# A six-layer decoder on one core: sigmoids ahead in the up pass, more key buffers in the product stage, and the end by token tiles

## The reference

```python
x = ln(x + linear_attention(x))
x = ln(x + cross_attention(x, ctx))
x = ln(x + ffn(x))
x = ln(x + metric_attention(x))          # causal, per head metric
x = ln(x + cosine_cross_attention(x, ctx))
x = ln(x + real(ifft(fft(x) @ w)) + bias)
# ffn: every qdq scales by the maximum of its whole tensor
x = act_qdq(x)
up = act_qdq(x @ w_up.T)                 # 256 -> 768
gate = act_qdq(x @ w_gate.T)
sig = round_u16(sigmoid(gate))
t = act_qdq(gate * sig)
v = act_qdq(t * up)
return v @ w_down.T
```

## Time and profile before

| | |
|---|---|
| Median of 3 runs | 1425.21 us (1424.16 to 1429.18) |
| The profiled execution | 1429.01 us, its span 1427.2 us |
| PE busy | 1249.9 us (88%), granted clock 0.95 |
| DVE, ACT, POOL busy | 1042.0 (73%), 516.8 (36%), 263.7 us (18%) |
| DMA | 107.86 MB, mean 76 GB/s |

### The profile page before, as it was taken

One profiled execution on the slowest core, in us unless ns is written; L12 is line 12 of the kernel. 1 busy time (PEld: TensorE's weight loads), 2 busy tenths in 40 slices (PEclk: granted clock), 3 DMA queues, 4 the chain that ended last, 5 costly groups with the idle time before them and its releaser, 6 DMA issues.

```text
span 1427.2 us, 18392 instructions
## 1 busy us (share of the span) xinstructions
PE 1249.9 (88%) x7324; PEld 832.9 (58%) x7324; DVE 1042.0 (73%) x1930; ACT 516.8 (36%) x605; POOL 263.7 (18%) x184
## 2 busy tenths in 40 slices
PE   7899999979899999722778999999999999998964
PEld 4465666656544544311555676867768686766553
DVE  3579889986345598996343687978878797968684
ACT  1334434434434567674011333332323323341320
POOL 0011111110000000043100321414142231414140
PEclk9999999999999999856889999999999999999998
DMA  5001000004651246495221110121111100000000
GB/s 211 15 16 31 30 31 30 16 15 126 210 199 59 74 167 216 154 391 178 86 96 54 44 52 31 33 73 37 59 54 52 39 15 28 26 24 23 1 15 15
DMA packets 47781, 107.86 MB, mean 76 GB/s; under 512 B 10704, under 2 KB 31312, under 8 KB 44240
## 3 DMA queue, kind: packets, MB, share of 16 engines
q1 hardware_dynamic: 43536, 104.59, 21.0%
q10 hardware_dynamic: 4160, 2.10, 0.5%
HBM read 62.64 MB, written 44.04 MB: 75 GB/s over the span
## 4 chain that ended last, share of the span: by engine, by line
PE 74%; DVE 15%; ACT 4%; issue 3%; DMA 2%; POOL 1%; SPq 0%; POOLq 0%; DVEq 0%; ACTq 0%
PE ps L1290 8%; PE ps L1350 7%; PE ps L1177 6%; PE ps L1025 6%; PE ps L1076 6%; PE ps L779 3%; PE ps L1323 3%; PE ps L1237 3%; PE ps L927 2%; PE ps L1261 2%; PE ps L852 2%; PE ps L1272 2%; PE ps L1367 2%; PE ps L870 2%; PE ps L1337 2%
## 5 line engine op out<-in xcount | busy, mean ns | idle before, releaser
L1350 PE MATMUL ps<-arena 128*128 128x256 f32 x512 | 120.0, 388 | 6.7 <-ACT arena L1775 6.7
L1290 PE MATMUL ps<-arena 128*128 128x512 f32 x256 | 117.6, 598 | 0.0
L1350 PEld LDWEIGHTS ps<-arena 128*128 128x128 f32 x512 | 98.5, 195 | 28.0 <-ACT arena L1775 10.2
L1802 POOL TENSOR_TENSOR arena<-arena 128x4 f32<-128x4 f32 x48 | 49.4, 1033 | 340.7 <-DVE arena L1957 340.7
L2283 DVE TENSOR_TENSOR arena<-ps,arena 128x2048 f32<-128x2048 f32 x32 | 73.3, 2291 | 41.5 <-PE ps L1237 41.0
L1863 POOL TENSOR_TENSOR arena<-arena 128x16 f32<-128x16 f32 x32 | 91.9, 2908 | 34.1 <-DVE arena L2312 34.1
L1177 PE MATMUL ps<-arena 128*128 128x256 f32 x384 | 89.3, 392 | 9.0 <-DVE arena L2236 6.7
L1177 PEld LDWEIGHTS ps<-arena 128*128 128x128 f32 x384 | 74.7, 197 | 20.2 <-issue 7.1
L1025 PE MATMUL ps<-arena 128*128 128x512 f32 x192 | 85.5, 602 | 1.2 <-ACT arena L1502 1.2
L1076 PE MATMUL ps<-arena 128*128 128x512 f32 x192 | 84.7, 595 | 0.0
L1290 PEld LDWEIGHTS ps<-arena 128*128 128x128 f32 x256 | 46.3, 190 | 48.2 <-issue 44.5
(11 more groups left out here) (262 smaller groups left out, 2621.8 us busy)
## 6 DMA issues: line engine op xcount, KB each, us to landing
v_scratch<-arena SPq DMA_DIRECT2D x7, 1536.0 KB, 12.7
arena<-v_scratch SPq DMA_DIRECT2D x7, 1536.0 KB, 6.8
up_scratch<-arena SPq DMA_DIRECT2D x6, 1536.0 KB, 7.3
arena<-up_scratch SPq DMA_DIRECT2D x6, 1536.0 KB, 10.2
vw_scratch<-arena SPq DMA_DIRECT2D x32, 256.0 KB, 3.9
arena<-x_scratch SPq DMA_DIRECT2D x16, 512.0 KB, 4.4
arena<-vw_scratch SPq DMA_DIRECT2D x8, 1024.0 KB
arena<-x SPq DMA_DIRECT2D x8, 512.0 KB, 5.3
```

The lines of the kernel that those rows point to most:

```text
L1290: last = mm(flat(p % 2), w["cos_wq"][:, k, p * P:(p + 1) * P], xt4[:, k], start=k == 0, stop=k == NC - 1)
L1350: last = mm(flat(2)[:, C:2 * C], cos_pt[:, p], cos_vw[:, par, p], start=p == 0, stop=p == NP - 1)
L1802: g.tensor_tensor(var[0], var[1], neghalf[:, 0:NT], ALU.pow)\
```

## The change

In the up pass, ACT rounds gate n and takes its sigmoid between the early and the late copies of up batch n - 1; before, the rounding came after the late copies and the sigmoid between the copies of batch n. Copies of value products move later, 13 to 15 into the product stage. The peak of t is taken ahead of that of up; the last up peak is taken in two halves.

In the product stage keys get three rows (the first over the value weights, no longer needed), a square in the same place, four staging tiles and PSUM banks of their own (`KEY_BANK`); the waits on `ck_stored` go from ACT, and POOL waits for all four before it clears the pads. ACT's and SP's orders change. The partition maximum of v is found by PE and DVE: DVE spreads the maximum over 128 columns, PE transposes them, DVE takes the maximum of a row.

In loop two's last batch, everything behind `cos_o_add` is done tile by tile, with four stores of 128 KB.

```diff
         late_ctx = ar.take(NC, B * TC)
         assert ar.at <= weights + 2 * NC * FF
         ar.at = keep + V_ORDER[0] * NF * T
-        krow = ar.take(2, INNER)
-        ksq = ar.take(INNER)
+        krow = [wv_all[:, 0:INNER], ar.take(INNER), ar.take(INNER)]
+        ksq = wv_all[:, INNER:2 * INNER]
+        spread = vst[:, 0:P]
+        kst = [ar.take(NP, P)]
         ar.at = keep + V_ORDER[1] * NF * T
-        kst = ar.take(NP, P)
+        kst += [ar.take(NP, P) for g in range(3)]
+        KEY_BANK = (1, 3, 6, 1)
...
+            load_up(2)
+            store_vw(13)
+            load_up(3)
+            store_v(0)
             store_vw(14)
-            load_up(2)
-            load_up(3)
-            store_vw(15)
-            store_v(0)
+            store_v(1)
             load_up(4)
-            store_v(1)
             load_up(5)
             store_v(2)
+            store_vw(15)
             load_up(6)
             store_v(3)
...
+                if b.last():
+                    for t in range(NT):
+                        wait_tile(sp, "y6_ready", t)
+                        sp.dma_start(out_rows[B - 1][:, t], y6[:, t]).then_inc(sig("y_stored", 16).sem, 16)
+                    return
...
-                if g >= 2:
-                    pe.wait_ge(ev("cos_k_scaled"), g - 1)
+                if g == 2:
+                    pe.wait_ge(ev("vw_copied"), 2 * NP)
+                if g == 3:
+                    pe.wait_ge(ev("cos_k_scaled"), 1)
...
+                        last = mm(flat(KEY_BANK[g] + half), late_ctx[:, k, g * P:(g + 1) * P],
...
             value_products(14)
-            value_products(15)
             key_rows(0)
             key_rows(1)
+            value_products(15)
+            key_rows(2)
             turn_keys(0)
-            key_rows(2)
             turn_keys(1)
             key_rows(3)
             turn_keys(2)
             turn_keys(3)
-
-
-            pe.wait_ge(ev("vw_copied"), 2 * NP)
+            pe.wait_ge(ev("cos_k_scaled"), 4)
+            pe.wait_ge(ev("peak_found"), QUANTIZED["v"])
+            tr(flat(7)[:, 0:P], spread, ident).then_inc(ev("peak_shared"), 1)
...
+            def last_turn(t):
+                wait_tile(pe, "y5_ready", t)
+                for c in range(NC):
+                    last = tr(flat(4 + t)[:, c * P:(c + 1) * P], y5[:, t, c * P:(c + 1) * P], ident)
+                last.then_inc(sig("cos_x_turned").sem, 1)
+
+            def last_spec(t):
+                wait_tile(pe, "cos_x_copied", t)
+                for k in range(NC):
+                    last = mm(flat(SPEC_BANK[t])[:, 0:C], xt5[:, k, t * P:(t + 1) * P], spec_m[:, k],
+                              start=k == 0, stop=k == NC - 1)
+                last.then_inc(sig("spec_done").sem, 1)
...
+                wait(pe, "cos_pt_copied", b, NT, NT)
+                last_turn(0)
+                last_turn(1)
+                wait(pe, "cos_scaled", b, NT, NT)
+                last_spec(0)
+                last_turn(2)
+                last_spec(1)
+                last_spec(2)
+                last_turn(3)
+                last_spec(3)
...
+                if b.last():
+                    last_rows(b)
+                    return
...
             gate_round(1)
+            ffn_sigmoid(1)
             ffn_copy_up(0, late)
             copy_spec_forward()
             ffn_copy_up(1, early)
-            ffn_sigmoid(1)
+            gate_round(2)
+            ffn_sigmoid(2)
             ffn_copy_up(1, late)
-            gate_round(2)
             copy_spec()
             ffn_copy_up(2, early)
-            ffn_sigmoid(2)
+            gate_round(3)
+            ffn_sigmoid(3)
             ffn_copy_up(2, late)
...
             ffn_copy_up(3, early)
-            ffn_sigmoid(3)
+            gate_round(4)
+            ffn_sigmoid(4)
             ffn_copy_up(3, late)
             copy_vw(8)
-            gate_round(4)
+            ffn_copy_up(4, early)
+            gate_round(5)
+            ffn_sigmoid(5)
+            ffn_copy_up(4, late)
             copy_vw(9)
...
             copy_vw(10)
-            gate_round(6)
+            ffn_copy_up(6, early)
+            gate_round(7)
+            ffn_sigmoid(7)
+            ffn_copy_up(6, late)
...
             copy_vw(12)
-            copy_vw(13)
...
-                if g == 0:
+                if g == 1:
                     act.wait_ge(moved("v_stored", 0), moved_before("v_stored") + 16)
                     wait(act, "v_ready", Batch(1))
-                if g >= 2:
-                    act.wait_ge(ev("cos_k_turned"), g - 1)
-                f(krow[:, g % 2], flat(1 + 2 * (g % 2), 2), ACT.Copy).then_inc(ev("cos_k_copied"), 1)
+                if g == 3:
+                    act.wait_ge(ev("cos_k_turned"), 1)
+                f(krow[g % 3], flat(KEY_BANK[g], 2), ACT.Copy).then_inc(ev("cos_k_copied"), 1)
...
-                f(ksq, flat(1 + 2 * (g % 2), 2), ACT.Square).then_inc(ev("cos_k_squared"), 1)
...
                     wait(act, "v_ready", Batch(2))
-                else:
-                    act.wait_ge(ev("ck_stored"), 16 * g)
-                f(kst.rearrange("p a b -> p (a b)"), flat(1 + 2 * (g % 2), 2), ACT.Copy, scale=gk)\
+                f(kst[g].rearrange("p a b -> p (a b)"), flat(KEY_BANK[g], 2), ACT.Copy, scale=gk)\
...
+                act.dma_start(ck_d[:, :, g * P:(g + 1) * P], kst[g]).then_inc(ev("ck_stored"), 16)
...
             copy_values(7)
+            ffn_round_up(0)
+            copy_vw(13)
+            ffn_round_up(1)
+            ffn_round_t(1)
+            copy_keys(0)
             copy_vw(14)
-            ffn_round_up(0)
-            ffn_round_up(1)
-            copy_vw(15)
-            ffn_round_t(1)
             ffn_round_up(2)
             ffn_round_t(2)
-            copy_keys(0)
             ffn_round_up(3)
+            copy_vw(15)
+            copy_keys(1)
             ffn_round_t(3)
             ffn_round_up(4)
-            copy_keys(1)
+            copy_keys(2)
             ffn_round_t(4)
             ffn_round_up(5)
             ffn_round_t(5)
             store_keys(0)
             ffn_round_up(6)
-            copy_keys(2)
             ffn_round_t(6)
             store_keys(1)
+            copy_keys(3)
             ffn_round_up(7)
-            copy_keys(3)
             ffn_round_t(7)
             store_keys(2)
             store_keys(3)
...
+                if b.last():
+                    wait_previous(act, "spec_done", b)
+                    for t in range(NT):
+                        wait_tile(act, "cos_x_turned", t)
+                        f(xt5[:, :, t * P:(t + 1) * P], flat(4 + t)[:, 0:C].rearrange("p (c n) -> p c n", c=NC), ACT.Copy)\
+                            .then_inc(sig("cos_x_copied").sem, 1)
+                    return
...
+            share_peak("t")
             share_peak("up")
-            share_peak("t")
...
-            share_peak("v")
 
 
             wait_all_moved(pool, "v_stored", 4, 3)
+            pool.wait_ge(ev("ck_stored"), 16 * 4)
...
+            def last_rstd(name, t):
+                rs = norms[name][2][:, t:t + 1]
+                wait_tile(pool, name + "_stats", t)
+                g.tensor_tensor(rs, rs, neghalf[:, 0:1], ALU.pow).then_inc(sig(name + "_rstd").sem, 1)
...
+                    if b.last() and t:
+                        last_rstd("cos", t - 1)
...
+                    last_rstd("cos", NT - 1)
...
+                if b.last():
+                    for t in range(NT):
+                        last_rstd("spec", t)
...
+                if name == "v":
+                    link(v.tensor_reduce(quant["v_all"], flat(7)[:, 0:P], AX.X, ALU.max))
...
+            def last_up_peak():
+                for n in range(2):
+                    wait(dve, "up_copied", Batch(B - 1), NF * (n + 1) // 2, NF)
+                    half = ffn_up[:, (B - 1) % 2].rearrange("p t j n -> p t (j n)")[:, :, n * FF // 2:(n + 1) * FF // 2]
+                    v.memset(spare, 0.0)
+                    link(v.tensor_reduce(quant["tmp"], half, AX.XY, ALU.max, apply_absolute_value=True))
+                    last = v.tensor_tensor(quant["up_max"], quant["up_max"], quant["tmp"], ALU.max)
+                    if n == 0:
+                        link(last)
+                last.then_inc(sig("up_peaked").sem, 1)
+                wait(dve, "up_peaked", Batch(B - 1))
...
-            up_peak(B - 1)
-            peak("up")
             t_peak(B - 1)
             peak("t")
+            last_up_peak()
+            peak("up")
+            scale("t", quant["t_raw"])
             scale("up", quant["x_scale"])
-            scale("t", quant["t_raw"])
...
-                if q in (2, 3, 5, 6):
-                    sum_keys((2, 3, 5, 6).index(q))
-            peak("v")
+                if q in (1, 2, 3, 5):
+                    sum_keys((1, 2, 3, 5).index(q))
+            v.tensor_copy(spread, quant["v_max"].broadcast_to([P, P])).then_inc(ev("peak_found"), 1)
...
+            def last_stats(name, t, rows):
```

(69 more changed lines are left out.)

28 lines of the change are left out of this document (11 added, 17 removed).

## The result

The changed kernel takes 1405.09 us (median of 4 runs, 1404.13 to 1406.1) against 1425.29 us on the same chip: ratio 0.9856, 95% interval 0.9838 to 0.9873, some 20.5 us. The forecast was 1398.7, range 1393 to 1406: the time lies inside, 6.4 us above the forecast. The profiled execution took 1406.1 us with a span of 1404.2.

A forecast was written before the change was run, and what follows sets the result against it. The prediction saw PE 88% busy, with holes in the product stage and the last 26 us. Gains of 16.4 us up to scale v and 10.1 at the end, taken from the median 1425.2, gave 1398.7 us, range 1393 to 1406.

The forecast's parts named there:

- What bounds the kernel: PE is busy 88% of the span; gains outside the loops come from two holes, product stage and last 26 us.
- Sigmoids ahead: Up pass: DVE no longer waits for sigmoids but 12.6 us for late copies; up scale at 590.0, gain 3.3 us.
- wait some 0.75 us each: Up pass: value products 9 and 11 wait for a vw copy; PE ends at 583.3, before DVE wants it (586).
- the block on ACT stops PE: Up pass rival, 4%: each of seven blocks of rounding and sigmoid stalls PE 5.5 us; time 1440.
- First product: Start of the product stage: at 592.8 against 597.6, a gain of 4.8 us that includes the sigmoids' 3.3.
- Product stage: First product to last v peak: 65.3 us for 61.6 of DVE work, ending at 658.1, with 1.5 for late loads.
- The rival on transfers: Product stage, 18%: full DMA engines set the pace, loads come 5 us behind, stage ends at 663; time 1404.
- keys only a symptom: Product stage rival, 5%: stage stays DMA-full and doesn't shorten; peak path and end alone give 13.5 us, 1411.7.
- Peak of v: End of the product stage: new path 1.0 us plus 0.85 for the scale, scale v at 660.0; peak path gains 3.4.
- The end: Loop two's last batch by tiles: span's end at 1417.1, a gain of 10.1 us, bounds 6 to 12.
- The sum: Whole kernel: gains of 16.4 and 10.1, together 26.5 us, taken from the median 1425.2, give 1398.7 us.

The follow-up runs named there:

- experiments 1 and 2: The kernel before and the changed kernel, each run and profiled once more without any edit: 1423.83 us and 1404.99 us.
- experiment 4: The kernel before with only the product stage of the change (key buffers, orders, vw copies, peak of v): 1416.0 us, ratio 0.9933.
- Experiment 3: The kernel before with only the up pass of the change, vw copies 13 and 14 still ahead of the first rounding: 1429.39 us, ratio 1.0027.
- experiment 8: The changed kernel loading only half of each of six up batches in the product stage (v not the reference's): 1404.88 us, stage 64.8 us.
- experiment 9: The changed kernel with one staging tile for scaled keys instead of four, each scaling waiting for the store before: 1414.0 us, ratio 0.9911.
- Experiment 6: The changed kernel with the maximum of v taken by POOL's all-reduce again instead of DVE, PE, DVE: 1402.94 us, ratio 0.9845.

## Why the prediction was right, and where it was not

- **What bounds the kernel:** right. Of the 25.7 us, 21.9 came from the two holes and 3.8 from the end of the up pass; loop two kept its length to 0.1 us.
- **Sigmoids ahead, gain 3.3 up to the scales:** 2.5 in the profiled execution (DVE's waits 13.1 us for 12.6), from the later scale before to the later one after. In the other four traces with this up pass and the moved vw copies it was 0.9, 0.9, -0.7 and -2.3 us, because of PE's clock behind the pauses at value products 9 and 11. The step that failed is "wait some 0.75 us each ... PE then ends at 583.3, still before DVE wants it". The times in it are right where no clock is lost: PE's last up product ended 109.35 us after the rounding of gate 0, walked 109.5. But the waits come on top of pauses of 1.69 us and make them 2.37, and I gave them no price in clock; that is 0 to 4.9 us (experiments 1 and 2). The rival "the block on ACT stops PE" had PE stop at the late copies, where it never stopped. So as ordered here the sigmoids brought nothing in the mean: the first product came 1.5 us earlier over the five traces, and the moved vw copies alone gave 2.1 (experiment 4, one trace). With late and vw copies first the same idea gave 5.0 more than experiment 4.
- **First product, 4.8:** 3.8, and 2.2 in the second trace; right in kind. It counted the 3.3 from the later scale (593.3), but ACT's first rounding waits for the up scale, which came first before the change (592.4). Experiment 3 shows that it hangs on the vw copies.
- **Product stage, 65.3 us:** mis-sized, 67.2 in both traces. Late loads cost 2.4, not 1.5 (experiment 8). What remains there, 64.8 for DVE's 61.6, are two one-column maxima of 1.33 us that I had at 0.16 (2.3 us) and 0.9 for a rounding of t; the loads' part shows on DVE as a key sum 1.5 us late for its square and 0.9 more for t. The mechanism, key stores out of ACT's way, was right (experiment 9). The rival on transfers has the right sign and half the size; "keys only a symptom" is out.
- **Peak of v, 1.85 us:** 2.07, and the gain of 3.3 as forecast, but for a wrong reason. I took the 3.9 us ahead of the all-reduce as its price. Experiment 6 shows that they go as soon as POOL's keys end early.
- **The end, 10.1:** 12.4, over the upper bound of 12. The last small store is 1.2 us shorter, which I had left out, and my walk was 1.1 us long: y5(3) was ready 6.2 us behind `cos_out(3)`, not 6.9, and the rest went behind it. The cost of splitting is real, 0.42 for a tile against 1.22 for four at once, and the overlap pays for it many times. The Trainium skill's advice on small tiles (VectorE: DVE Perf Modes, The TRN2 errata) would have kept the four tiles together; here the trace speaks against it, with 13.8 us for 26.2.
- **The sum.** By stages I was 0.8 us off in the profiled execution. The rest of the 6.4 us is in the base: I took a difference read in one execution of 1429.01 us from a median 3.8 lower. The trace of before was itself a slow one, partly in the very stage that the change shortens (73.46 against 71.72), and the trace of after lost 2.7 us before the change begins. From the means of two traces each, 1426.4 and 1405.5, the change is 20.9 us: start -2.5 (luck), first product 3.0, product stage 5.4, peak 3.2, the end and what lies behind the span the remaining 12.

## What to carry to other kernels

When an order is moved on one engine, list for every other engine the longest pause it now makes, and not only the sum of waits: a pause that is covered in time can still lower TensorE's clock behind it, and two edits of order (late copies and vw copies first) were worth 6 us on top of the change's 20. A staging buffer that waits for a store among full transfers holds up whatever stands behind it on that engine: of a landing of 15.4 us ACT stood 9.2, and the stage grew by 10.5. Before a gain read in one trace is taken from a median, see how the profiled execution stands to it, and in which stage.

## What the runs showed of the hardware

- TensorE's clock can fall behind a pause of 2.37 us: the granted clock was 0.56 in the 3 us behind it in the trace of experiment 6, near the low level of 1.2 GHz, and 1.00 in the same place of the first trace of the changed kernel. It fell behind six of twelve such pauses, behind both of 4.4 us, and behind none of 1.69. The Trainium skill (TensorE: Matmul & The Clock Gate, Part 1: The HAM clock gate) says that the number of instructions at low clock differs between runs of one kernel; the traces agree, with 0 to 4.9 us of cost in an up pass.
- The same code up to the start of the up pass differed by up to 3.1 us between two executions of one kernel, and by up to 5.7 us over all fourteen traces, with a granted clock of 1.00, 0.97 or 0.91 in its first 60 us.
- POOL's all-reduce began 5.8 to 6.1 us after POOL's last multiply in four traces, or 0.14 us after the peak when 7.3 us had passed (two traces).
- A one-column maximum on DVE took 1.33 us instead of 0.16 beside a multiply of 128x1024 elements on POOL, and ended with it.
